# A fused attention and expert layer: the last chunk in three groups instead of two

## The reference

```python
h = layernorm(x) * (1 + ca) + sa
x = x + ga * attention(h)              # softmax over all earlier keys, then w_proj
h = layernorm(x) * (1 + cb) + sb
g = sigmoid(h @ gate_w.T); topv, topi = top_k(g, 4)
combine[token, topi] = topv / sum(topv)
routed = sum_e (silu(h @ e_win[e]) * (h @ e_vin[e]) * combine[:, e]) @ e_wout[e]
shared = (silu(h @ ws_in) * (h @ vs_in)) @ ws_out
x = x + gb * (shared + routed)
```

## Time and profile before

| what | value |
|---|---|
| median of 3 runs | 419.4 us (417.22 to 419.75) |
| profiled execution, its own time | 418.65 us |
| its span, first to last instruction | 416.8 us |
| what lies around the span | 1.85 us |
| PE busy | 371.9 us (89%) |
| DVE busy | 273.3 us (66%) |
| ACT busy | 227.9 us (55%) |
| POOL busy | 92.3 us (22%) |
| chain that ended last | PE 63%, DVE 19%, ACT 6%, issue 5% |
| mean granted TensorE clock | 0.943 |

### The profile page before, as it was taken

How to read it: one execution, slowest core, us unless ns; L and a number is a source line. 1 busy time by engine, 2 the same in 40 slices (tenths; PEclk the granted TensorE clock), 3 DMA queues, 4 the chain that set the end, 5 groups by cost and what they waited for, 6 DMA issues and landing times.

```text
span 416.8 us, 5984 instructions
## 1 busy us (share of the span) xinstructions
PE 371.9 (89%) x2091; PEld 178.1 (43%) x2091; DVE 273.3 (66%) x649; ACT 227.9 (55%) x425; POOL 92.3 (22%) x123
## 2 busy tenths in 40 slices
PE   7579989898999987998989969999999999788884
PEld 7255433343463443434544323343542543234463
DVE  4667864999967988853488326897769880141473
ACT  1310567556668743536844436876786554478332
POOL 6126403703200297001262000006004500010000
PEclk9855699999999996999999989999999999899999
DMA  8680418212304400630150000000054000003400
GB/s 193 103 115 9 53 15 200 49 27 52 78 1 106 101 2 0 135 71 6 35 62 2 2 2 25 2 2 1 1 113 95 2 0 2 25 0 57 99 0 27
DMA packets 23773, 19.46 MB, mean 47 GB/s; under 512 B 6768, under 2 KB 20496, under 8 KB 23744
## 3 DMA queue, kind: packets, MB, share of 16 engines
q1 hardware_dynamic: 23328, 18.69, 23.0%
q10 hardware_dynamic: 416, 0.39, 0.3%
HBM read 11.22 MB, written 1.17 MB: 30 GB/s over the span
## 4 chain that ended last, share of the span: by engine, by line
PE 63%; DVE 19%; ACT 6%; issue 5%; POOL 4%; DMA 2%; POOLq 0%; SPq 0%; DVEq 0%; ACTq 0%
PE bank L953 59%; DVE mn L838 10%; ACT pr L688 2%; DVE sl L943 1%; POOL xn L565 1%; PE bank L1129 1%; DMA qa<-qp 1%; POOL rstd L556 1%; ACT L688 1%; PE bank L990 1%; DVE xn L765 1%; ACT L692 1%; PE bank L1164 1%; ACT sl L692 1%; DVE y L863 1%
## 5 line engine op out<-in xcount | busy, mean ns | idle before, releaser
L838 DVE TENSOR_REDUCE mn<-bank 128x1 f32<-128x512 f32 (+3 forms) x304 | 185.1, 655 | 56.8 <-PE bank L953 56.3
L688 ACT ACTIVATE pr<-bank 128x512 f32<-128x512 f32 x288 | 160.4, 599 | 111.2 <-PE bank L953 109.7
L953 PE MATMUL bank<-ka,qa 96*128 96x128 bf16 (+3 forms) x576 | 113.1, 292 | 11.8 <-DVE mn L838 5.8
L953 PE MATMUL bank<-qa,ka 98*128 98x512 bf16 x288 | 109.8, 392 | 4.8 <-DMA qa<-shiftT 2.3
L953 PE MATMUL bank<-pr,va 128*32 128x512 f32 x576 | 79.8, 627 | 0.7 <-ACT pr L688 0.7
L953 PEld LDWEIGHTS bank<-ka,qa 96*128 96x128 bf16 x576 | 49.2, 104 | 63.6 <-DVE mn L838 27.8
L953 PEld LDWEIGHTS bank<-qa,ka 98*128 98x128 bf16 x288 | 28.0, 100 | 86.0 <-ACT pr L688 42.1
L953 PE MATMUL bank<-hT_parts,up_parts 128*128 128x512 f32 (+1 forms) x216 | 61.8, 416 | 1.2 <-ACT sl L692 1.0
L953 PEld LDWEIGHTS bank<-hT_parts,up_parts 128*128 128x128 f32 x216 | 39.1, 191 | 10.5 <-issue 1.8
L630 POOL TENSOR_TENSOR sl<-sl,comb_wide 128x512 f32<-128x512 f32 x24 | 29.9, 1277 | 61.4 <-ACT sl L692 32.9
L555 POOL TENSOR_SCALAR rstd<-mv 128x4 f32<-128x4 f32 (+2 forms) x9 | 2.1, 235 | 175.9 <-DVE mv L871 175.7
(11 more groups left out here) (140 smaller groups left out, 264.6 us busy)
## 6 DMA issues: line engine op xcount, KB each, us to landing
comb_wide<-comb_rows SPq DMA_DIRECT2D x6, 1024.0 KB, 9.6
qa<-q_marks SPq DMA_DIRECT2D x4, 768.0 KB, 6.2
qa<-qp SPq DMA_DIRECT2D x18, 128.0 KB
comb_wide<-comb_rows SPq DMA_DIRECT2D x2, 768.0 KB, 8.4
xs<-in_L_attn_x SPq DMA_DIRECT2D x4, 256.0 KB, 4.9
qa<-qp SPq DMA_DIRECT2D x12, 64.0 KB
out_x<-xs SPq DMA_DIRECT2D x3, 256.0 KB, 2.3
sl<-in_L_ffn_e_win SPq DMA_DIRECT2D x1, 512.0 KB, 3.9
```

Of the source, the lines that this page charges most:

```text
L688: act.activation(pr[:, n % NPB, g, :], s_bank[in_s[x] % NS][:, :], ACT.Exp, scale=SCALE).then_inc(s_read, 1)
L838: v.tensor_reduce(mn[:, place[u] % 2, part, h:h + n], m_bank[k % NM][:, 0:n * w].rearrange("p (n w) -> p n w", w=w), AX.X, ALU.max, negate ...
L953: return pe.matmul(out, lhsT, rhs, start=start, stop=stop, skip_group_check=True)
```

## The change

The last chunk is cut into three groups: `LAST` is now units 12 and 13 (256 columns), and units 14 and 15 are each a group of one, `SOLOS`, both with the tokens on the partitions; `END` is the second of them. The steps up_end, turn_end and down_end carry the group's name. Unit 14's steps are written by the planner's queues, with due times after its "h2": up_end i at 2.6 + 0.9 i, the multiplication by the shares (now a step of its own, "mix") after its last "pick", turn_end 0.8 after each mix, down_end 1.2 after the last. The "gate" of `LAST` goes from DVE to POOL as for the other chunks, its down is written two parts a step, and the part of the hand-written end that dealt with `LAST` is gone. Unit 14's turned tiles go through the m banks and are copied by DVE; unit 15's go through the s banks and ACT as before. Turned tiles are written back over `up_end`, and unit 14 works in `hT`.

```diff
-    END = NC
-    GROUPS = CHUNKS + [END]
-    group = {c: (c, 4 * c, 4) for c in CHUNKS} | {LAST: (LAST, 4 * LAST, 3), END: (LAST, 4 * LAST + 3, 1)}
+    SOLOS = [NC, NC + 1]
+    END = SOLOS[-1]
+    GROUPS = CHUNKS + SOLOS
+    group = {c: (c, 4 * c, 4) for c in CHUNKS} | {LAST: (LAST, 4 * LAST, 2)}
+    group |= {c: (LAST, 4 * LAST + 2 + i, 1) for i, c in enumerate(SOLOS)}
...
         elif kind == "h2" and a != END:
             side.append((now + (1.6 if turn_of[a] < 3 else 0.9), ("h2_split", a)))
             smalls.append((now + 1.6, ("route", a)))
-            st["h_ready"][turn_of[a]] = now + (5.0 if turn_of[a] < 3 else 2.5)
+            if a in SOLOS:
+                side.extend((now + 2.6 + 0.9 * i, ("up_end", a, i)) for i in range(EP))
+            else:
+                st["h_ready"][turn_of[a]] = now + (5.0 if turn_of[a] < 3 else 2.5)
         elif kind == "h2":
-            plan.extend([("h2_split", a), ("route", a)])
-            for f in range(1, FC + 1):
-                for q in (side, vins):
-                    for y in [y for y in q if y[1] in (("gate", LAST, f), ("vin", LAST, f))]:
-                        q.remove(y)
-                        plan.append(y[1])
-                        if y[1][0] == "gate":
-                            vins.append((now, ("vin", LAST, f)))
-                        else:
-                            plan.append(("down", LAST, f - 1))
-            plan.extend([("up_end", 0), *(("pick", a, i) for i in range(4)), *(("up_end", i) for i in range(1, EP))])
-            plan.extend([("down", LAST, FC), ("gated", LAST), ("turn_end", 0), ("turn", LAST)])
-            plan.extend([*(("turn_end", i) for i in range(1, ET)), ("down_end",)])
+            plan.extend([("h2_split", a), ("route", a), ("up_end", a, 0), *(("pick", a, i) for i in range(4))])
+            plan.extend(("up_end", a, i) for i in range(1, EP))
+            for i in range(ET):
+                plan.extend([("mix", a, i), ("turn_end", a, i)])
+            plan.append(("down_end", a))
...
+        elif kind == "pick" and a in SOLOS:
+            side.extend((now + 1.8 + 0.9 * i, ("mix", a, i)) for i in range(ET))
+        elif kind == "mix":
+            side.append((now + 0.8, ("turn_end", a, x[2])))
+        elif kind == "turn_end" and x[2] == ET - 1:
+            smalls.append((now + 1.2, ("down_end", a)))
...
         elif kind == "gate":
-            vins.append((now + (1.7 if a != LAST else 0.2), ("vin", a, x[2])))
-        elif kind == "vin" and a == LAST:
-            if x[2]:
-                plan.append(("down", LAST, x[2] - 1))
+            vins.append((now + (1.7 if a != LAST else 1.0), ("vin", a, x[2])))
...
-            plan.append(("down", c, f))
-            st["down"] = (c, f + 1)
-            if f == FC:
+            n = min(FC + 1 - f, 1 if c != LAST else 2)
+            plan.extend(("down", c, f + i) for i in range(n))
+            st["down"] = (c, f + n)
+            if f + n > FC:
...
-                elif kind == "gate" and x[1] != LAST:
+                elif kind == "gate":
                     c, f = x[1:]
+                    w = width[c]
                     gp.wait_ge(comb_in[c], 32)
                     gp.wait_ge(s_read, in_s["hin", c, f] + 1)
-                    gp.tensor_tensor(sl[:, f, :], sl[:, f, :], comb_wide[:, f - 1, :], ALU.mult).then_inc(gated_up, 1)
+                    gp.tensor_tensor(sl[:, f, 0:w], sl[:, f, 0:w], comb_wide[:, f - 1, 0:w], ALU.mult).then_inc(gated_up, 1)
...
                 elif kind == "up_end":
-                    i = x[1]
+                    c, i = x[1:]
                     fs = slice(2 * i, min(2 * i + 2, FC + 1))
+                    if c != END:
+                        act.wait_ge(h2_parts, 3)
                     act.wait_ge(m_ready, in_m[x] + 1)
-                    act.activation(up_end[:, fs, :], end_bank(x)[:, :, 0, :], ACT.Silu).then_inc(end_silu, 1)
+                    act.activation(up_end[c][:, fs, :], end_bank(x)[:, :, 0, :], ACT.Silu).then_inc(end_silu, 1)
...
+                elif kind == "turn_end" and x in in_m:
+                    c, i = x[1:]
+                    fs = slice(4 * i, min(4 * i + 4, FC + 1))
+                    v.wait_ge(m_ready, in_m[x] + 1)
+                    v.tensor_copy(up_end[c][:, fs, :].rearrange("p f m -> p (f m)"),
+                                  turn_bank(x)[:, 0:P * (fs.stop - fs.start)]).then_inc(m_read, 1)
```

More of the change, by code:

```diff
@@ L93, in adaln_attention_moe_kernel @@
     LEAD = 9
-    SPACE = {"shift": 1.3, "oT": 1.7, "yT": 1.2, "proj": 1.4, "h2": 1.6, "route": 1.3, "combT": 1.3, "turn": 1.5, "gates": 1.3,
+    SPACE = {"shift": 1.3, "oT": 1.7, "yT": 1.2, "proj": 1.4, "h2": 1.6, "route": 1.3, "combT": 1.3, "turn": 1.5, "gates": 1.3, "down_end": 0.5,
              "hT": 1.6, "q": 2.6, "k": 2.6, "v": 1.2, "gated": 0.0}
-    RANK = ("shift", "gates", "proj", "yT", "oT", "hT", "q", "k", "v", "h2", "route", "combT", "turn", "down")
+    RANK = ("shift", "gates", "proj", "yT", "oT", "hT", "q", "k", "v", "h2", "route", "combT", "turn", "down_end", "down")
     plan = []
@@ L304, in adaln_attention_moe_kernel @@
     at, use, uses = {}, {}, [0] * 2
-    late = [("oT", order[-1]), ("yT", order[-1]), ("proj", order[-1]), ("h2", END), ("route", END), ("down_end",)]
+    late = [("oT", order[-1]), ("yT", order[-1]), ("proj", order[-1]), ("h2", END), ("route", END), ("down_end", END)]
     for n, x in enumerate(plan):
@@ L313, in adaln_attention_moe_kernel @@
             early_uses = uses[1]
-    in_s = {x: n for n, x in enumerate(x for x in plan if x[0] in ("scores", "hin", "turn_end"))}
-    in_m = {x: n for n, x in enumerate(x for x in plan if x[0] in ("max", "vin", "up_end"))}
-    gate_no = {x: n for n, x in enumerate(x for x in plan if x[0] == "gate" and x[1] != LAST)}
+    in_s = {x: n for n, x in enumerate(x for x in plan if x[0] in ("scores", "hin") or x[:2] == ("turn_end", END))}
+    in_m = {x: n for n, x in enumerate(x for x in plan if x[0] in ("max", "vin", "up_end", "turn_end") and x not in in_s)}
+    gate_no = {x: n for n, x in enumerate(x for x in plan if x[0] == "gate")}
     norms = [x for x in plan if x[0] in ("norm", "norm2")]
+    vector_norms = [("norm", c0), ("norm", c1), ("norm2", LAST), *(("norm2", c) for c in SOLOS)]
     norm_no = {x: n for n, x in enumerate(norms)}
@@ L379, in adaln_attention_moe_kernel @@
         osb = sb("osb", [P, 2, CH], f32)
-        up_end, down_end = (pr[:, i, :, :].rearrange("p g x -> p (g x)")[:, 0:(FC + 1) * P].rearrange("p (f m) -> p f m", m=P)
-                            for i in range(2))
-        out_end = pr[:, 0, 3, 0:D]
+        solo = {SOLOS[0]: hT[:, 0:3, :].rearrange("p c x -> p (c x)"), END: pr[:, 0, :, :].rearrange("p g x -> p (g x)")}
+        up_end = {c: solo[c][:, 0:(FC + 1) * P].rearrange("p (f m) -> p f m", m=P) for c in SOLOS}
+        out_end = {c: solo[c][:, (FC + 1) * P:(FC + 2) * P] for c in SOLOS}
         rec = sb("rec", [P, 2, H], f32)
@@ L502, in _ @@
                 elif kind in ("turn", "down_end"):
-                    c = x[1] if kind == "turn" else END
+                    c = x[1]
                     ov = out_d.rearrange("b (t p) d -> p (b t) d", p=P)
@@ L557, in _ @@
                     k = norm_no[x]
-                    if x not in (("norm", c0), ("norm", c1), ("norm2", LAST), ("norm2", END)):
+                    if x not in vector_norms:
                         gp.wait_ge(rstd_ready, k + 1)
@@ L756, in _ @@
                     ins.then_inc(stats_ready, 1)
-                elif x in (("norm", c0), ("norm", c1), ("norm2", LAST), ("norm2", END)):
+                elif x in vector_norms:
                     c, k = x[1], norm_no[x]
@@ L905, in _ @@
                                         tsum[:, 1, 0:n].unsqueeze(2).broadcast_to([P, n, E]), ALU.mult).then_inc(share_ready, 1)
[L906 to L911, removed]
@@ L912, in _ @@
                 elif kind == "up_end":
-                    i = x[1]
+                    c, i = x[1:]
                     fs = slice(2 * i, min(2 * i + 2, FC + 1))
[L915 to L918, removed]
+                    v.wait_ge(end_silu, EP * SOLOS.index(c) + i + 1)
+                    v.tensor_tensor(up_end[c][:, fs, :], up_end[c][:, fs, :], end_bank(x)[:, :, 1, :], ALU.mult).then_inc(m_read, 1)
+                elif kind == "mix":
+                    c, i = x[1:]
@@ L919, in _ @@
                     fs = slice(max(4 * i, 1), min(4 * i + 4, FC + 1))
                     e0, e1 = EC * (fs.start - 1), EC * (fs.stop - 1)
[L921 to L924, removed]
+                    v.wait_ge(share_ready, turn_of[c] + 1)
@@ L925, in _ @@
+                    v.wait_ge(m_read, in_m["up_end", c, (fs.stop - 1) // 2] + 1)
+                    part = up_end[c][:, fs, :].rearrange("p f (s m) -> p (f s) m", m=F)
+                    v.tensor_tensor(part, part, eg[:, units(c).start, e0:e1].unsqueeze(2).broadcast_to([P, e1 - e0, F]),
                                     ALU.mult).then_inc(end_mixed, 1)
```

(21 more changed lines are left out.)

36 lines of the change are left out of this document (20 added, 16 removed).

## The result

The change makes the kernel slower: 437.5 us (median of 4 runs) against 418.4, ratio 1.0449, 95% interval 1.0405 to 1.0494. The profiled execution took 437.09 us with a span of 435.3, against 418.65 and 416.8. So the forecast had the direction, but little more than half the size: +10.3 us forecast, +18.4 us between the two profiled executions.

A forecast was written before the change was run, and what follows sets the result against it. No engine was taken as full in unit 15's attention, and behind it unit 15's own chain decides. Evac +15.7 and tail -5.4 give +10.3 us on 418.65: 429.0 us, range 422 to 435.

The forecast's parts named there:

- ACT's stretch: In unit 15's attention: five lone Silus among Exps, ten more table loads (12.8 us), 17.8 us of ACT without pause.
- The tail: Behind unit 15's evac: its chain runs alone without LAST's work, -5.4 us, from -6.4 to -3.4.
- The term for it: In the tail: PE's lower clock between small steps gives back 1.0 us, bounds 0 and 3.
- The walk before and behind the stretch: Step-by-step times through unit 15's attention, around ACT's stretch, putting unit 15's evac at 406.0 for 390.3: +15.7 us.
- The last part: Behind ACT's stretch, up to unit 15's evac: sixteen attention steps plus moved PE work, 16.2 us.
- The step that failed: Under unit 14's blocks: moved norm2, h2, route, pick and combT of LAST, 3 us on DVE, cost 0, uncovered up to 2.
- The bound of PE in the attention: At the end of unit 15's attention: PE is the bound, so moved downs, down_end, vins and transposes add 5.5 us.
- Silus get together: Rival for ACT's stretch: one pair of loads or hidden loads, PE's 8.9 us decide, 420.0 us, no change; chance 0.07.
- A switch costs the load: Rival on ACT's table switches: each of ten costs two load lengths, 12.8 us more, 441.8 us; chance 0.03.
- the "faster" rival: Rival for unit 15's attention: moved work falls into PE's 7.0 idle us and loads are covered, 417.4 or 414; chance 0.05.

The follow-up runs named there:

- e1: Changed kernel with unit 14's five Silus made Exps, order untouched, so the ten added table loads are gone: 427.2 us, ratio 1.0200.
- e2: Changed kernel with unit 14's five up_end due at the same time, two loads in place of ten: 429.9 us, ratio 1.0225.
- e5: Changed kernel; LAST's hin await unit 14's h2, its up_end follow; units 12 and 13's chain behind the previous chunk's last max step and gate: 422.1 us, 1.0087.
- e6: e5 plus thirteen identity matmuls, result unread, between unit 15's yT, proj and h2: ratio 1.0102.
- e3: Changed kernel with norm2 of units 12 and 13 on POOL and not on DVE: 434.8 us, ratio 1.0350.
- e7: Changed kernel with the edits of e1 and e3 together: 424.3 us, ratio 1.0134.
- e8: Kernel before the change with only the eight gates of LAST (384 columns) on POOL and not on DVE: ratio 1.0039.

## Why the prediction was wrong

The direction and the mechanism with the largest price, the table loads, were right. The time was 8 us longer than forecast and left the range (435), because a stage that I had costed at nothing was not free.

- **ACT's stretch**: forecast 17.8 us, ten loads, ACT without a pause; measured 17.9, ten loads, ACT 98% busy. One step of the planner's order was off (up_end 0 behind the fourth step of block 66, not the third, and up_end 4 behind the first of block 68), which left the length of the stretch as it was. Runs e1 and e2 save 9 to 10 us, e1 by removing the ten loads alone, e2 by moving the up_end together.
- **The tail**: forecast -5.4 from 26.5; measured -6.0. The clock fell where I had said (0.83 over the tail). The term for it was too high: I took 1.0 us, and e5 against e6 gives 0.3 for the up_end.
- **The walk before and behind the stretch**: from unit 14's evac to the stretch 17.1 forecast, 17.6 measured. The last part 16.2 forecast for sixteen steps, 18.1 measured for fifteen: at least 1.9 too little. I had only summed work, and PE idles 2.7 us in it, 1.32 of them at down_end for ACT's fT (408.23).
- **The step that failed** is "DVE's 3 us for them stand beside PE-bound work; I cost this at 0 (cover: PE full there; without it up to 2)". I had unit 14's evac at 354.9, 1.7 us earlier than before; it came at 361.27. Against a stage of 29.2 us there were 36.7: 7.5 us. The cover was named wrongly. PE was busy 30.73 of 30.91 us there, but its banks are given free by DVE's max and vin: the wait of 2.85 us ends with DVE's vin at L952. Work put on DVE ahead of them became idle time of PE, though in the kernel before DVE was busy for only 15.7 us of this stage. I had listed norm2 among what is moved, and did not ask, for it, what is queued behind it and which engine releases it. Of the 7.5 us, 3.0 to 4.1 go with norm2 on another engine (e3 and e7: PE's idle time of 2.85 us and the half clock behind it are gone). e5, with the whole chain written behind the max steps, has this stage back to 1.1 us more than before. What is left between the two is the combT that waits for pick with the downs behind it, the order of h2 and its split among the max steps, and h2's own work; no run takes these apart.
- **The bound of PE in the attention.** I had it right that moved work is paid there. e5 puts the number on it: +8.8 us for 9.3 us of PE's work, against 6.3 in the tail.
- **The rivals**: "Silus get together" would have given 420.0 by my sum; made real, it gives 429.9 and 427.0, since the other stage's 6 us were not in it. A switch costs the load of 1.28 us and 0.03 us around it and no more, in the changed kernel too; the "faster" rival is out, as even e5 is 0.9% slower.

Sum of the misses: 7.5 + 0.5 + 0.1 + 1.9 - 0.6 (tail) - 1.2 (the start, which is scatter between executions) = 8.2, which is 18.5 less 10.3.

## What to carry to other kernels

Before an activation is moved between others, count the table loads that its new neighbours make; keep activations of one table together, even when their inputs then have to wait a block. A stage in which PE is 99% busy is no cover for DVE work if DVE is who frees PE's banks: look at what stands behind the new instruction in its queue, and at whom it waits for. And the idle time of PE in a stage is no room for moved work until a run shows it: here 9 us of PE's work lengthened a stage with 7 us of idle time by 9 us, for 6 us less of tail.

## What the hardware showed that I had not expected

DVE instructions that read and write SBUF alone stretch to the end of the POOL instruction beside them. The two tiles of norm2 (tensor_scalar) took 1.21 and 1.30 us beside gates of 1.27 us, and 0.34 us each with POOL idle; the cast of h2_split took 1.26 us and 0.29 us. In e8, where the gates of 384 columns take POOL 0.99 us, the single tile of unit 15 took 0.95 us for 0.35 and its cast 0.73 for 0.23. One tensor_tensor with both inputs in SBUF (the shares, L923 in e5) took 0.61 us for 0.19. Each of them ends 0.03 to 0.15 us behind the end of a gate. DVE's multiplications and reductions with an input in PSUM kept their 0.69 and 0.68 us beside the same gates. The Trainium skill's page "SBUF — State Buffer" (section "SBUF: two separate sides") says that DVE and GpSimd share one pair of ports as "an exclusive lock, not a bandwidth split", held for a whole instruction; the traces of this case agree. No run here tells which property of the DVE instruction draws it in.
